# Second layer norm and queries of a cross attention moved into its programs, and segment attention as rounds that overlap

## What is computed

```python
# layer 0, 16 heads of 8 channels
x1 = layernorm(x) @ sa_wqkv ; self attention (causal) ; r = x + sa_out
xq = layernorm(r, ln2) ; xs = layernorm(context, ln2)
q2 = xq @ ed_wq ; k2, v2 = xs @ ed_wkv
r = r + softmax(q2 k2^T / sqrt(128)) v2 @ ed_wproj
r = r + relu(layernorm(x, ln3) @ ff_w1 + b1) @ ff_w2 + b2
# layer 1, 16 heads of 64 channels, segments of 64 tokens (56 are there)
pooled = rms_norm(context.mean(tokens)) ; k_extra, v_extra from pooled
q, k, v = rms_norm(r) @ to_qkv ; q, k = rope(q), rope(k)
o = softmax([k_extra, persist, k] . q, causal) [v_extra, persist, v]
r = r + o @ to_out ; r = r + (silu(g) * a) @ ff_w2 + b2      # a, g from rms_norm(r) @ ff_w1
```

## Time and profile before

| | us |
|---|---|
| median of 3 runs | 1302.47 (1302.31 to 1303.64) |
| the profiled execution | 1302.12 |
| its span, first to last instruction | 1300.3 |
| mean granted TensorE clock | 0.937 of 2.4 GHz |

### The profile page before, as it was taken

One profiled execution on the slowest core, in us unless ns is written; L12 is line 12 of the kernel. 1 busy time (PEld: TensorE's weight loads), 2 busy tenths in 40 slices (PEclk: granted clock), 3 DMA queues, 4 the chain that ended last, 5 costly groups with the idle time before them and its releaser, 6 DMA issues. The chain is left out here.

```text
span 1300.3 us, 38106 instructions
## 1 busy us (share of the span) xinstructions
PE 1129.7 (87%) x15980; PEld 769.9 (59%) x15980; DVE 905.0 (70%) x1734; ACT 742.1 (57%) x1025; POOL 837.2 (64%) x1235
## 2 busy tenths in 40 slices
PE   1999558999999999999999999997576978879775
PEld 1556444666666666666666666665444747366472
DVE  6788647878787877778787877766367363765632
ACT  1344434777777777777777777776323425353341
POOL 3465488887887878787887878740058284773720
PEclk9999768999999999999999999999986988989985
DMA  7200033223232323232232323110000000000000
GB/s 172 77 1 1 2 110 117 78 97 100 82 101 86 108 66 121 74 103 94 82 115 72 107 80 107 52 49 26 18 0 2 2 8 2 1 9 1 8 2 8
DMA packets 70407, 76.01 MB, mean 58 GB/s; under 512 B 21308, under 2 KB 64956, under 8 KB 70108
## 3 DMA queue, kind: packets, MB, share of 16 engines
q1 hardware_dynamic: 70236, 73.57, 18.0%
HBM read 32.89 MB, written 0.92 MB: 26 GB/s over the span
## 5 line engine op out<-in xcount | busy, mean ns | idle before, releaser
L976 DVE TENSOR_REDUCE tops_sb<-ps_b 112x2 f32<-112x1000 f32 x384 | 460.5, 1199 | 157.6 <-PE ps_b L826 154.7
L922 ACT ACTIVATE probs_sb<-ps_a 128x896 f32<-128x896 f32 x352 | 322.6, 917 | 117.6 <-PE ps_a L807 117.6
L798 PE MATMUL ps_d<-probs_sb,values_sb 128*32 128x112 f32 x6144 | 226.8, 265 | 1.0 <-ACT probs_sb L922 1.0
L826 PE MATMUL ps_b<-keys_sb,queries_sb 64*112 64x500 f16 x768 | 164.4, 419 | 17.1 <-DVE tops_sb L976 10.6
L217 POOL TENSOR_SCALAR context_sb<-context_sb,ln_sb 125x128 f32<-125x128 f32 x384 | 167.4, 455 | 7.6 <-POOL ln_sb L235 7.5
L798 PEld LDWEIGHTS ps_d<-probs_sb,values_sb 128*32 128x32 f32 x6144 | 134.1, 109 | 40.2 <-issue 6.7
L807 PEld LDWEIGHTS ps_a<-queries_sb,keys_sb 64*128 64x128 f16 x3072 | 124.6, 102 | 49.7 <-ACT probs_sb L922 9.0
L807 PE MATMUL ps_a<-queries_sb,keys_sb 64*128 64x112 f16 x3072 | 140.2, 209 | 6.2 <-ACT probs_sb L922 6.0
L854 PE MATMUL ps_c<-xs_t_sb,w_kv_sb 128*128 128x200 f32 (+1 forms) x384 | 127.2, 430 | 0.0
L863 PE MATMUL ps_c<-w_kv_sb,xs_t_sb 128*128 128x128 f32 x768 | 120.9, 295 | 5.3 <-ACT k_rows_sb L939 5.3
L741 POOL TENSOR_TENSOR k_split_sb<-k_rows_sb,k_split_sb 128x500 f16<-128x500 f32 x96 | 109.1, 1136 | 8.0
(11 more groups left out here) (254 smaller groups left out, 1853.8 us busy)
## 6 DMA issues: line engine op xcount, KB each, us to landing
keys_sb<-k_split_sb SPq DMA_DIRECT2D x288, 125.0 KB, 2.2
context_sb<-in_ctx SPq DMA_DIRECT2D x32, 750.0 KB
queries_sb<-q_split_sb SPq DMA_DIRECT2D x24, 112.0 KB, 5.8
keys_sb<-in_ones SPq DMA_DIRECT2D x3, 375.0 KB, 5.2
w_qk_sb<-in_w_qkv SPq DMA_DIRECT2D x1, 1024.0 KB, 11.5
queries_sb<-shift_sb SPq DMA_DIRECT2D x64, 1.8 KB
x_all_sb<-in_x SPq DMA_DIRECT2D x2, 448.0 KB
queries_sb<-in_zeros SPq DMA_DIRECT2D x8, 112.0 KB, 5.6
```

The lines of the kernel that those rows point to most:

```text
L798: last = nc.tensor.matmul(o_bank[32 * (g % 4):32 * (g % 4) + 32, 112 * (g // 4):112 * (g // 4) + 112], values[r][:, k, g, :], probs[k % 2] ...
L826: last = nc.tensor.matmul(ps_b[0:2 * T, 512 * e:512 * e + 500], queries_of(b + d, e, g), keys[(r + d) % 3][64 * e:64 * e + 64, g, 500 * u: ...
L922: nc.scalar.activation(probs[s % 2][:].rearrange("p (e n) -> p e n", e=2), halves(ps_a[:, :]), ACT.Exp).then_inc(Q["probs_ready"], 1)
L976: nc.vector.tensor_reduce(tops[(b + d) % 2][:, :, n // 3, n % 3], ps_b[0:2 * T, :].rearrange("p (e n) -> p e n", e=2)[:, :, 0:500], axis=A ...
```

## The change

**Self attention.** Layer norm, transposes and queries leave the block. GpSimd works on the first two context tiles inside the loop: sums of tile 0 at the end of iteration 0, deviation and rows of tile 0 in iteration 1, sums and deviation of tile 1 in iteration 2, its rows in iteration 3. VectorE counts tile 0 at the end of iteration 0 (and no longer ahead of the loop), tile 1 at the end of iteration 1, and then the statistics of `r1` for pairs 0 to 7 and 8 to 11, with the reciprocal root of these twelve in iteration 3 ahead of `rows_done`.

**Cross attention.** The rows come in groups q of four pairs. Group 0 is normalised on VectorE as the block's first work, transposed in step -3 and multiplied in step -2; groups 1 to 3 are normalised on ScalarE (in step -2, with scale and bias) and go through TensorE, ScalarE and VectorE in step -1, three places s each. `ps_d` holds them one after the other. The low half is spread by ScalarE and no longer by VectorE. The intermediate tiles lie in `values[2]` and `keys[2]`, so the fills of these tiles move to step 0. `load_queries` now waits for the halves of its group, and the first one stands in SP's program behind the first three key DMAs. The three transposes of context 1 stand together at s = 8 of step -2, and the scans of sequence 0 alternate between `ps_b` and `ps_a`.

**Segment attention.** `passes` goes. In front stand the 16 projections of group 0 with their values. Then round i has the scores of group i (with four of its eight value products between those of the first half, for i > 0), and 16 steps n, in which TensorE projects group i + 1, transposes and weights group i, runs the MLP of group i - 1, and in steps 14 and 15 projects the output of group i. After round 3 follows the MLP of group 3. The projections use two PSUM banks and no longer four. The rms norm of the MLP is cut in four pieces, at n = 0 to 3. All of its instructions stay.

```diff
+                        if i % 2 == 0:                       # GpSimd, self attention
+                            b = i // 2
+                            pool.wait_ge(context_in[b], 16)
+                            context_sums(pool, b, b)
...
+                        if i % 2 == 1:
+                            b = i // 2
...
+                            context_normed(b)
...
+                        if i < 2:                            # VectorE, self attention
+                            context_counted(i)
+                        else:
+                            rows_counted(2 * U * (i - 2), U * i)
...
                     def load_queries(n):
 
+                        sp.wait_ge(A["q_high_out"], NQ * n // (2 * U) + 1)
+                        sp.wait_ge(A["q_low_out"], NQ * n // (2 * U) + 1)
...
+                                if b == -2 and u == 0:
+                                    load_queries(0)
...
+                            wait("best_ready", d, n - (b + d == 0))
...
+                    for i in range(NIT):                     # TensorE, segment attention
...
+                                scores(i, half, u)
+                                if i > 0 and half == 0:
+                                    values1(i, u // 2, u % 2)
+                        for n in range(16):
+                            if i + 1 < NIT:
+                                projected(i + 1, n)
+                            late = LATE_VALUES.get(n, ()) if i > 0 else ()
+                            for u, half in late[:1]:
+                                values1(i, u, half)
+                            for u, part in TURNED.get(n, ()):
+                                turned(i, u, part)
+                            for u, half in late[1:]:
+                                values1(i, u, half)
+                            for u, half in WEIGHTED.get(n, ()):
+                                weighted(i, u, half)
+                            if i > 0:
+                                mlp(i - 1, n)
+                            for u in OUT.get(n, ()):
+                                out(i, u)
+                    for n in range(16):
+                        mlp(NIT - 1, n)
...
+                    for i in range(NIT):                     # VectorE, segment attention
+                        softmax(i)
+                        if i + 1 < NIT:
+                            memory_keys(i + 1)
+                        for n in range(16):
+                            if i + 1 < NIT:
+                                rotate(i + 1, n)
+                            if i > 0:
+                                mlp_normed(i - 1, n)
+                                mlp(i - 1, n)
```

More of the change, by code:

```diff
@@ L725, in emit @@
                         wait = waiter(pool, b, r)
[L726 removed]
+                        norm = has(3) and b + 3 > 1
                         if norm:
@@ new lines, in mlp_down @@
+                    def mlp_down(i):
+                        wait = waiter3(pe, i)
+                        wait("up_ready", 3)
+                        for u in range(U):
+                            for m in range(3):
+                                last = nc.tensor.matmul(banks[6][:, 128 * u:128 * u + 128], gate_e[:, m, 128 * u:128 * u + 128],
+                                                        w_down1[:, m, :], start=(m == 0), stop=(m == 2))
+                        last.then_inc(R["down_done"], 1)
@@ L1495, in total, with softmax @@
+                    def softmax(i):
+                        wait = waiter3(ve, i)
+                        link, ends = main[i]
                         def total(u):
```

704 lines of the change are left out of this document (405 added, 299 removed).

## The result

The change takes 1289.99 us (median of four runs, 1287.43 to 1291.88) where the kernel before takes 1302.44: a ratio of 0.9897, with an interval of 0.9881 to 0.9914. That is 12.5 us and not the 33 that were forecast, and it lies above the stated range. The profiled execution took 1288.46 us, with a span of 1286.5.

What follows compares the result with a forecast made beforehand. Chains around the cross attention steps, which TensorE fills, were taken to bound the kernel. From a span of 1300.3 us, 21.2 for self attention and ramp and 12.1 for segment attention gave 1267.0, so 1269 measured; range 1251 to 1285.

Steps and rivals of the forecast that it cites:

- +1.45 twice: Self attention iterations 0 and 1: 2.42 us of statistics ahead of the next `k_wide`, less VectorE's spare 0.97 us.
- the 1.3 and the nothing that follow it: Self attention: statistics and aggregations ending iteration 2 cost +1.3 us; those of iteration 3 fit in 3.50 us of waiting.
- self attention pays: Rival, chance 0.05: GpSimd's context work beside VectorE's two-input SBUF operations costs 4 us in all; total 1273.
- the bound of 20: Ramp: first scan +20 us after the block's start if keys, not queries, come last; +23.2 was forecast.
- 9.1 us of gain: Ramp, first scan to first scores: two PSUM banks remove waits of 0.76 us from twelve VectorE scans.
- 2.9 us for `hn_ready`: Full rounds, step 4: new wait of 2.9 us, `mlp_turned` and TensorE's work behind it waiting for the norm.
- 3.3 for the held operations: Full rounds: eleven small norm operations held beside GpSimd's rotations cost VectorE 0 to 11 us; 3.3 reaches TensorE.
- the old cold stretch: Segment attention: half-speed transposes after the old 4.40 us wait, clock 0.50; not taken off, since rounds have three such waits.
- the 3.7 us of waits ahead of step 2: Full rounds: new 3.7 us wait because two banks wait for VectorE and ScalarE right after the softmax.
- full rounds stay at 79: Rival, chance 0.12: `hn_ready` and half clock eat the overlap in rounds 1 and 2, only outer rounds gain; 1275.
- slower: Rival, chance 0.04: TensorE falls to 1.2 GHz after three waits per round and stays there for much of it; about 1331.
- fraction: Self attention iteration 1: GpSimd's context work exceeds its 10.6 us of idle time by a fraction, covered by VectorE's own shift.

Runs made afterwards that it cites:

- counts_spread: The change with VectorE's statistics of context and rows moved from the end of self attention iterations into its two waits; 1284.1 us, ratio 0.9837.
- one_bank: The change with all scans of sequence 0 in one PSUM bank pair, as before the change; 1294.0 us, ratio 0.9911.
- warm_6: The change with six unread products on TensorE in its wait for the norm at step 4, rounds 1 and 2; 1285.7 us, ratio 0.9877.
- dealt: The change with self attention statistics in VectorE's waits, norm, attention pieces and MLP steps dealt out anew, round 3's MLP earlier; 1263.1 us, ratio 0.9695.

## Why the prediction was wrong, step by step

| term (us) | forecast | measured |
|---|---|---|
| start of the cross attention | 146.0 | 151.97 |
| to the first scan | 23.2 | 20.2 |
| to the first scores | 26.5 | 30.0 |
| steps | 714.5 | 716.9 |
| head of segment attention | as before, 52.8 | 52.4 |
| first scores read to last residual | 266.5 | 278.4 |
| tail | 37.6 | 36.8 |

The span is 19.5 us longer than forecast, and the largest part of that, 11.9, is in the rounds. What failed above all is the price of the half clock behind a wait of TensorE, in the rounds and in the larger part of self attention.

**Self attention (+6.0).** The step that failed is "+1.45 twice" with the 1.3 and the nothing that follow it. The statistics themselves cost what was forecast: 2.4 us gained and three times 1.3 lost, +1.5 in all. The sum priced VectorE's delay by its own clock alone. The delay also changed who starts first on the key spreading, which takes VectorE 0.3 to 0.7 us longer in each iteration (2.3 in all), and gave TensorE a wait of 2.6 us; in three of the four iterations its products behind the start of the scores run slower (0.7, 1.6 and 1.6). `counts_spread` shows it for the second and the third iteration. The rival "self attention pays" had 4 us for this place, but by another mechanism, VectorE's operations held beside GpSimd's context work. That one no row shows. But GpSimd's context work is not hidden everywhere either, against the forecast: not in the fourth iteration of `counts_spread`, and not in the case shown at the end of this section.

**Ramp (+0.5 in sum).** Two errors nearly cancel, and that is luck. The first scan comes 3.0 us sooner after the start of the cross attention than forecast: the chain of the queries was counted too long, and the bound of 20, where the keys come last, was the right value. To the first scores it is 3.5 us more. The waits of VectorE were taken as 9.1 us of gain, from a row that holds for five of twelve scans; `one_bank` shows 2.7.

**Steps (+2.4).** They were not free. From the first scores to the end of step 0 it is 25.0 us and was 23.4, and step 1 takes 23.1 for 22.5; from step 2 on they are equal. The first part is again the clock. The first windows of step 0 in the changed kernel:

```profile
202.10:208.09 5.99, 5.99 (x66) 3.25 (x63) 3.00 (x3) 3.18 (x5) 3.97 (x9) 0.57 0.51 151
208.09:227.20 19.11, 18.99 (x314) 13.09 (x311) 15.74 (x30) 14.47 (x21) 15.86 (x28) 1.00 0.35 104
```

TensorE enters the steps at half clock, with a key product of 1.03 us that takes 0.61 before, where the clock was 1.00 from the first scores on. This is the 1.6 us of step 0. The clearing that moved into step 0 stands at 225.7, behind that stretch, and delays the scans by the 0.6 us of step 1. It was priced at nothing, or at 2 us if its cover failed; the cover failed, for 0.6. The forecast had no term for the clock at this place.

**Rounds (+11.9).** From the first read of scores round 0 was forecast at 57.1 and takes 59.9; the full rounds, forecast at 76, take 78.5 each; round 3, forecast at 57.4, takes 61.5. For the full rounds the mechanism was named and its wait nearly right: 2.9 us for `hn_ready` and 3.3 for the held operations make 6.2, and the wait is 5.79. What failed is the price of the clock behind it. The sum left the old cold stretch in and gave the new waits none. With the wait filled, in `warm_6`, a full round takes 74.1 us, so the clock costs 4.4 in the profiled round, 2.7 of them surely behind this wait. All other terms together were 1.9 us too long, for one because the 3.7 us of waits ahead of step 2 are 1.6; so that the error is 2.5 and not 4.4 is in part luck.

The two outer rounds make up more than half of the 11.9. In round 0 TensorE waits 2.83 us for the softmax and 2.21 for a bank, and transposes behind them take 1.45 to 1.98 us for 1.04; the clock of the round is 0.86. In round 3 the waits are 3.79 and 3.10, and behind the second the down product takes 4.57. `dealt`, without the second, is 2.6 us shorter there. For round 0 no kernel tried this alone, so the clock as the cause is read from its rows and not shown.

So the rival "full rounds stay at 79", which had a chance of 0.12, was right on the full rounds and on the mechanism. Its 1275 kept the forecast's outer rounds of 57 and its ramp, and both were too short. The rival "slower" had the right cause and the wrong size: the clock fell behind the wait of 5.79 us, as `warm_6` shows, and in most rounds at the down product, but not behind the 1.97 ahead of the first transposes (1.09 us), and not for half of a round.

**A term with several sizes.** The range allowed for ends of terms, but not for a term that comes in several sizes. In eight profiles of kernels with the changed self attention the cross attention starts between 151.3 and 156.4. VectorE and GpSimd in the third iteration of one of them, `one_bank`, and TensorE behind them:

```profile
88.90 6.36 DVE L596 TENSOR_TENSOR k_wide_sb<-k_sb,const_sb 128x512 f32<-128x512 f32 x2
...
88.07 6.04 POOL L500 TENSOR_TENSOR k_wide_sb<-k_sb,const_sb 128x512 f32<-128x512 f32 x6
...
95.41 1.99 PE L367 MATMUL ps_a<-k_wide_sb,q_sb 64*64 64x512 f32 x8 [6.10 <-DVE k_wide_sb L596]
```

Here the first of VectorE's two operations is held until all six of GpSimd's are over, TensorE waits 6.10 us and its clock falls, and the iteration takes 34.0 us. In the profiled execution of the change the same iteration takes 28.7 us. The eight profiles fall into two groups of four. In one, GpSimd has been idle for 0.3 to 1.0 us when the keys come, and VectorE takes 2.82 us. In the other GpSimd goes from the context rows straight into the keys, because the second iteration was short (28.7 us) and its context work ends too late, and VectorE takes 6.34 to 6.40. So the "fraction" by which iteration 1 (the second one) overruns GpSimd's idle time, which the forecast called covered, can cost 5 us. That it is the missing pause which shuts VectorE out is read from these eight profiles and was not tried. The change has one profile, so whether this is where its runs get their spread of 1287 to 1292 from is not shown either. In four kernels with the statistics spread the cross attention starts between 145.5 and 146.4.

## What to carry to other kernels

Before overlapping two chains that share TensorE, list its waits after the edit and add to each what its clock will cost behind it: here a wait of 5.8 us cost between 2.7 and 4.4 more, and the last 1.4 to 2.1 us of waiting in a round returned between 2 and 6. The price is no constant: rounds of the same program differ by up to 3 us. A norm that moves next to GpSimd's work was best dealt out in pieces that TensorE's work of their step covers. Delaying one of two engines that start together can hand the other the first turn, and here that cost more than the delay. When you hide work in an engine's idle time, follow the case in which everything before it runs fast, too: that is when it ends too late.

## What the runs showed of the hardware

VectorE's operation on 128x4 elements takes 0.16 us alone and up to 1.00 beside GpSimd's rotation. The scaling with one input and a column of scalars takes 2.51 us for four there, and 0.87 alone. The Trainium skill (SBUF — State Buffer, "Who interferes with whom") counts this kind among those that can contend; these rows agree. What I had not expected is that VectorE may wait through GpSimd instructions that follow each other without a gap: its two key operations took 1.29 us with GpSimd elsewhere, 2.14 when both engines started together, 2.82 when GpSimd was 1.2 us ahead, and 6.36 when GpSimd came to its six without a pause and was 0.8 us ahead.

The clock: a wait of 1.96 us was followed by the down product at 2.94 us in some rounds and at 4.2 to 4.6 in others, with the same instructions ahead of it. When it falls there could not be told from these runs.
